# Projection, norm and router of layer one between the rounds of the second attention, a batch behind it

## The reference, cut to what matters

```python
scores = jnp.where(causal[None, None], scores, -jnp.inf)
...
attn = jax.nn.softmax(scores, axis=-1)
out = jnp.einsum('bhqk,bhkd->bqhd', attn, v).reshape(B, T, C)
return out @ w_out
...
x = _layernorm(x + _L1_attn_ref(x, ...), axis=-1)
...
xn = _rmsnorm(x_flat, norm_weight, EPS)
logits = xn @ router_weight.T + router_bias
probs = jax.nn.softmax(logits, axis=-1)
gate_vals, expert_idx = jax.lax.top_k(probs, TOP_K)
...
oh = jax.nn.one_hot(e_flat, E, dtype=jnp.int32)
pos = jnp.sum(jnp.cumsum(oh, axis=0) * oh, axis=-1) - 1
keep = pos < CAP
```

## Time and profile before

| | us |
|---|---|
| median of three runs | 2147.64 (2146.42 to 2150.34) |
| the profiled execution, its own time | 2137.1 |
| its span | 2135.4 |
| PE, DVE, ACT, POOL busy (share of the span) | 86%, 72%, 54%, 24% |
| mean granted clock of PE, share of full | 0.921 |

### The profile page before, as it was taken

How to read it: one execution, slowest core, us unless ns; L and a number is a source line. 1 busy time by engine, 2 the same in 40 slices (tenths; PEclk the granted TensorE clock), 3 DMA queues, 4 the chain that set the end, 5 groups by cost and what they waited for, 6 DMA issues and landing times. The chain is left out here.

```text
span 2135.4 us, 34245 instructions
## 1 busy us (share of the span) xinstructions
PE 1830.3 (86%) x12608; PEld 1134.4 (53%) x12608; DVE 1535.8 (72%) x2490; ACT 1149.6 (54%) x2279; POOL 511.6 (24%) x600
## 2 busy tenths in 40 slices
PE   5675899999999999699999879999987646999970
PEld 3342333333333333388888745555546535899860
DVE  7998999999999995366676455555526764666636
ACT  2330588888888889522322125555545543544526
POOL 3552152100000000132231112222211552333323
PEclk9995799999999999899999969999998757999985
DMA  3855437655334401123453374665624413443406
GB/s 120 240 204 131 110 55 186 189 140 85 66 52 81 71 13 39 59 71 99 148 149 109 138 183 109 140 150 140 174 86 150 146 65 120 141 140 126 153 28 232
DMA packets 165277, 258.19 MB, mean 121 GB/s; under 512 B 18398, under 2 KB 94083, under 8 KB 165136
## 3 DMA queue, kind: packets, MB, share of 16 engines
q1 hardware_dynamic: 137184, 191.11, 35.2%
q0 software_dynamic: 11696, 33.62, 4.3%
q10 hardware_dynamic: 16256, 31.59, 4.2%
HBM read 145.30 MB, written 108.92 MB: 119 GB/s over the span
## 5 line engine op out<-in xcount | busy, mean ns | idle before, releaser
L845 DVE TENSOR_REDUCE b_mx<-b_PM 128x2 f32<-128x1024 f32 x512 | 620.9, 1225 | 17.3 <-PE b_PM L701 13.5
L813 ACT ACTIVATE b_probs<-b_PS 128x512 f32<-128x512 f32 x1024 | 551.2, 598 | 79.3 <-PE b_PS L749 41.5
L1686 DVE TENSOR_REDUCE d_mx<-d_PM 128x2 f32<-128x1024 f32 (+1 forms) x192 | 178.1, 956 | 133.1 <-PE d_PM L1531 82.4
L1652 ACT ACTIVATE d_probs<-d_PS 128x512 f32<-128x512 f32 (+3 forms) x384 | 163.9, 498 | 150.9 <-PE d_PS L1579 150.5
L701 PE MATMUL b_PM<-b_kst,b_qst 48*128 48x512 f32 x512 | 185.0, 446 | 0.0
L749 PE MATMUL b_PS<-b_qst,b_kst 50*128 50x512 f32 x512 | 183.6, 454 | 0.7 <-ACT b_probs L813 0.7
L726 PE MATMUL b_PO<-b_probs,x_v 128*32 128x256 f32 x2048 | 164.9, 394 | 2.1 <-ACT b_outT L803 0.6
L726 PE MATMUL b_PO<-b_probs,b_vst 128*32 128x256 f32 x2048 | 163.2, 391 | 2.8 <-ACT b_outT L803 1.6
L2428 ACT ACTIVATE f_h<-f_PH,w_b 128x512 f32<-128x512 f32 x96 | 66.2, 689 | 139.5 <-PE f_PH L2387 129.2
L1626 POOL TENSOR_SCALAR_AFFINE_SELECT d_probs<-d_probs 128x128 f32<-128x128 f32 x256 | 71.8, 292 | 269.5 <-ACT d_probs L1652 262.8
L749 PEld LDWEIGHTS b_PS<-b_qst,b_kst 50*128 50x128 f32 x512 | 76.8, 184 | 108.4 <-ACT b_probs L813 92.3
(11 more groups left out here) (276 smaller groups left out, 3913.8 us busy)
## 6 DMA issues: line engine op xcount, KB each, us to landing
halves<-a_parts SPq DMA_DIRECT2D x7, 2048.0 KB, 8.5
qk<-c_halves ACTq DMA_DIRECT2D x7, 2048.0 KB
w_w<-L_ffn_fc1T SPq DMA_DIRECT2D x12, 1024.0 KB
w_w<-L_ffn_fc2T SPq DMA_DIRECT2D x12, 1024.0 KB, 5.5
d_qst<-qk SPq DMA_DIRECT2D x36, 256.0 KB, 5.1
d_kst<-qk SPq DMA_DIRECT2D x36, 256.0 KB, 7.2
slots<-b_zero POOLq DMA_DIRECT2D x16, 516.0 KB
v<-a_vaug ACTq DMA_DIRECT2D x32, 256.0 KB, 3.5
```

What stands on the lines that cost most here:

```text
L813: act.activation(probs[:, s % RING], PS[bank(s)][:], ACT.Exp).then_inc(exped, 1)
L845: dve.tensor_reduce(mx[:, :, p, qt, kh], PM[t % MTILES][:], AX.X, ALU.max)\
L1652: act.activation(probs[:, s % RING, 0:w], PS[bank(s)][:, 0:w], ACT.Exp).then_inc(exped, 1)
L1686: dve.tensor_reduce(mx[:, :, qt, kh], PM[t % MTILES][:, :, 0:keys(qt, kh)], AX.X, ALU.max)\
```

## The change

`phase_route` is gone. A new class `Routing` holds its work, cut into 66 ticks for each batch (`TICKS`), and `phase_attention1` runs one tick of it behind each round, on every engine. Batch b is routed from the first round of group 4(b+1) on, so one batch behind the attention; a tick k of batch b stands behind round k mod 12. Batch 3 has no rounds beside it: its 66 ticks run after the last round, with the last 18 ticks of batch 2. Three things change besides the place:

- The heads are divided by their sums channel-major, without turning them. SP sends row 32 of each head from `outT` to `totals` (`load_totals`), DVE takes the reciprocal (`invert_totals`), SP stores it to a new array `shares1` (`store_shares`) and loads it back, spread over the 32 channels, beside the sums (`load`); then one multiplication (`weigh`, POOL for batches 0 to 2, DVE for the last) and the projection. The 16 plus 8 transposes of a block before the projection are gone.
- A whole batch goes through each step of the chain, so there are half as many steps, on tiles twice as wide. The running count is a scan over tiles.
- The router's products and transposes go through `PM`, the two tiles of the maxima. And there are three stacks of queries and keys in place of four (`BUFS = 3`); the expert weights are loaded ahead in groups 5, 6, 9 and 10 in place of 6, 8, 12 and 14.

```diff
-    BUFS = HG1
+    BUFS = 3
...
+    LATE_TOTALS = (10, 6)
-    FIRST_WEIGHTS = {6: (0, True), 8: (0, False), 12: (1, True), 14: (1, False)}
+    FIRST_WEIGHTS = {5: (0, True), 6: (0, False), 9: (1, True), 10: (1, False)}
...
+class Routing:
+    STEPS = 24
+    TICKS = 66
+    WEIGH, WEIGH_LAST = (16, 18), (16, 20)
+    PROJECT = (18, 20)
+    STATS = (19, 20, 21, 22)
+    AGGR = (23, 24)
+    VARIANCE, ROOTS, DEVIATION = 25, 27, 28
+    NORM = 29
+    TURN = (31, 33)
+    SEND_COPY = 31
+    LOGITS, EXPS, RANKS = 34, 36, 46
+    SCATTER = 50
...
+    def load_totals(self, sp, outT, g, half):
+        if g > 0:
+            sp.wait_ge(self.shares_out[half], 16 * g)
+        for j in range(G1):
+            rows = slice(j * P // G1, (j + 1) * P // G1)
+            sp.dma_start(self.totals[rows, half], outT[j * VS1 + D1:j * VS1 + D1 + 1, half]).then_inc(self.totals_in[half], 16)
+
+    def store_shares(self, sp, d, g, half):
+        sp.wait_ge(self.totals_made[half], g + 1)
...
+        sp.dma_start(d["shares1"][heads, tok].rearrange("h (c n) -> h c n", n=self.CUTS), self.totals[:, half])\
+          .then_inc(self.shares_out[half], 16)
+
+    def load(self, sp, d, n, out_stored):
+        b, i, tok = n // HPS, n % HPS, slice(n * BLK, (n + 1) * BLK)
+        sp.wait_ge(out_stored[i], 16 * ((b + 1) * HG1 + 1))
+        sp.wait_ge(self.shares_out[i], 16 * (b + 1) * HG1)
...
+        for c in range(CD):
+            heads = slice(c * self.HEADS, (c + 1) * self.HEADS)
+            sp.dma_start(self.sums[:, i, c], sums[heads, 0:D1, tok]).then_inc(self.sums_in[i], 16)
+            share = d["shares1"][heads, tok].unsqueeze(1).to_broadcast([self.HEADS, D1, BLK])
+            sp.dma_start(self.shares[:, i, c], share).then_inc(self.sums_in[i], 16)
+        sp.dma_start(self.x2[:, i], d["x2"][tok, :].rearrange("(t p) c -> p t c", p=P)).then_inc(self.x2_in[i], 16)
...
+    def multiply(self, pe, ident, b, k):
+        if k in self.PROJECT:
+            n = b * HPS + self.PROJECT.index(k)
...
+            pe.wait_ge(self.weighed, n + 1)
+            self.free(pe, "project", n)
+            for t in range(TPK):
+                for c in range(CD):
+                    mm = pe.matmul(out[:, t // 2, t % 2 * DIM:(t % 2 + 1) * DIM], self.sums[:, n % HPS, c, t * P:(t + 1) * P],
+                                   self.wout[:, c, :], start=(c == 0), stop=(c == CD - 1))
+            mm.then_inc(self.projected, 1)
...
+    def invert_totals(self, dve, g, half):
+        dve.wait_ge(self.totals_in[half], self.TOTAL_DMAS * (g + 1))
+        dve.reciprocal(self.totals[:, half], self.totals[:, half]).then_inc(self.totals_made[half], 1)
+
+    def weigh(self, eng, n):
+        i = n % HPS
+        eng.wait_ge(self.sums_in[i], self.SUM_DMAS * (n // HPS + 1))
+        eng.tensor_tensor(self.sums[:, i], self.sums[:, i], self.shares[:, i], ALU.mult).then_inc(self.weighed, 1)
...
+    def send(self, pool, d, b, k):
+        if b < BATCH - 1 and k in self.WEIGH:
+            self.weigh(pool, b * HPS + self.WEIGH.index(k))
+        if self.SCATTER <= k < self.SCATTER + TPB * TOP_K:
...
+            pool.indirect_dma_start(out=d["slots"], out_offset=bass.IndirectOffsetOnAxis(
+                ap=self.to_slot[:, t, c:c + 1].bitcast(U32), axis=0), in_=self.xn[:, t], in_offset=None,
+                bounds_check=SLOTS - 1, oob_is_err=False).then_inc(self.scattered, 16)
...
             load(1)
             rows(0)
-            for g in range(2, BUFS):
-                load(g)
+            load(2)
+            route.load_weights(sp, d)
             for g in range(GROUPS):
...
                 store(g, 0)
+                if g > 0:
+                    route.store_shares(sp, d, g - 1, 1)
                 if g + 1 < GROUPS:
                     rows(g + 1)
+                if g > 0 and g % HG1 == 0:
+                    for i in range(HPS):
+                        route.load(sp, d, g // HG1 * HPS - HPS + i, out_stored)
+                route.store_shares(sp, d, g, 0)
+                if g == GROUPS - 1:
+                    route.load(sp, d, BLOCKS - HPS, out_stored)
                 store(g, 1)
                 if g + BUFS < GROUPS:
                     sp.wait_ge(pv_done, (g + 1) * ROUNDS + RING // G1)
                     load(g + BUFS)
...
-            for g in range(GROUPS):
-                for i in range(ROUNDS):
-                    slot(g, i)
-            for r in range(ROUNDS - PAIRED, ROUNDS):
-                values(GROUPS - 1, r)
+            for T in range(TICKS):
+                if T < GROUPS * ROUNDS:
+                    slot(T // ROUNDS, T % ROUNDS)
+                if T == GROUPS * ROUNDS:
+                    for r in range(ROUNDS - PAIRED, ROUNDS):
+                        values(GROUPS - 1, r)
+                for b, k in Routing.at(T, PER_BATCH):
+                    route.multiply(pe, ident, b, k)
```

More of the change, by code:

```diff
@@ L1386, in phase_attention1 @@
+def phase_attention1(nc, d, keep, weights, tokens, shared):
     K = len(PAIRS1) * D1
     KM = K + HALVES1
-    BUFS = HG1
+    BUFS = 3
     GROUPS = BATCH * HG1
@@ L1425, in phase_attention1, with groups_left, maximum_at @@
     MASKS = masks_through(ROUNDS - 1)
+    def groups_left(g):
+        return min(2, GROUPS - 1 - g)
+    PER_BATCH = HG1 * ROUNDS
+    TICKS = GROUPS * ROUNDS + Routing.TICKS
+    def maximum_at(T):
+        if T < GROUPS * ROUNDS:
+            g, ahead, t = T // ROUNDS, 1 + (AHEAD + T % ROUNDS) // STEPS, (AHEAD + T % ROUNDS) % STEPS
+            if ahead <= groups_left(g):
+                return g + ahead, t
+    ring = [("max", 0, t) for t in range(STEPS)] + [("max", 1, t) for t in range(AHEAD)]
+    for T in range(TICKS):
+        if now := maximum_at(T):
+            ring.append(("max", *now))
+        for b, k in Routing.at(T, PER_BATCH):
+            ring.extend(Routing.entries(b, k))
+    entry = {name: n for n, name in enumerate(ring)}
     with ExitStack() as ctx:
@@ L2261 @@
-ROUTE_STEPS = 24
+            for T in range(TICKS):
+                if now := maximum_at(T):
+                    take(*now)
+                    if now[1] == STEPS - 1:
+                        minus_max(now[0])
+                g, i = T // ROUNDS, T % ROUNDS
+                if g < GROUPS and i == LATE_TOTALS[0]:
+                    route.invert_totals(dve, g, 0)
+                if 0 < g <= GROUPS and i == LATE_TOTALS[1]:
+                    route.invert_totals(dve, g - 1, 1)
+                for b, k in Routing.at(T, PER_BATCH):
+                    route.choose(dve, b, k)
@@ L2656, in program @@
             tokens = Routed(nc, layer1)
-            with ExitStack() as routing:
-                incoming = Unrouted(nc, routing)
-                phase_attention1(nc, d, keep, weights, incoming, shared)
-                phase_route(nc, d, keep, weights, incoming, tokens)
+            phase_attention1(nc, d, keep, weights, tokens, shared)
             phase_experts(nc, d, keep, weights)
```

852 lines of the change are left out of this document (368 added, 484 removed).

## The result

The changed kernel takes 2277.2 us (median of four, 2269.7 to 2279.9) against 2147.0 for the kernel before on the same chip. The ratio, its time over that of the kernel before, is 1.060, with a 95% interval of 1.057 to 1.063. It is slower by 130 us, where the forecast was 78 and the range ended at 2275. Its profiled execution took 2276.8 us, 139.7 more than that of before.

What follows compares the result with a forecast made beforehand. PE, busy 39.54 of 40 us in the attention rounds, was taken as the bound. Terms -187 + 82 + 41 + 82 + 43 + 17 = +78 took the profiled 2137.1 to 2215, so 2225 us was expected; range 2155 to 2275.

Steps and rivals of the forecast that it cites:

- The sign and its mechanism: Whole kernel: slower, chance 0.87, with PE waiting 13 times in round 6 for queries or keys and its clock falling.
- The rival in which the change is faster: Round 6 waits only 3.5 us each, 45 in all, too short to move the clock: -9, 2138 us; chance 0.12.
- the one in which the clock stays up: PE's clock does not fall after the round 6 waits: +35, 2182 us, still slower; chance 0.20.
- The rival in which the clock stays down: PE at half clock through most of each of 13 groups, losing 7.5 us instead of 3.3: 2280 us; chance 0.09.
- The removed stage, 187: phase_route, from PE's last value product to the experts' first load, disappears: -186.9 us.
- The tail, 82: Behind the last round, batch 3 is routed with nothing beside it: +82 us, bounds 72 to 92.
- Four loads issued at 0.6 and about 4 until 1 MB has landed: 6.4: Step of the tail: batch 3's loads ahead of the multiplication, 6.4 us.
- PE work, 41: Between the rounds, router projections, turns, logits and rank products take PE 13.8 us per batch, three batches: +41 us.
- Waits, 82: Round 6 of groups 3 to 15: PE waits 6.3 us for late queries and keys, 13 times: +82 us.
- Crowding, 17: Batch loads delaying keys (8), plus scatters and chain steps PE waits on in order (9): +17 us, bounds 0 to 30.
- 2 to 3 us late, three times: Step of crowding: keys delayed behind a batch's 3 MB, 13 us at 225 GB/s, in groups 4, 8 and 12: 8 us.
- The clock, 43: PE's clock falls after each of 13 round 6 waits, costing 3.3 us each: +43 us; bounds 0 to 4 each.

Runs made afterwards that it cites:

- spread loads alone: The changed kernel with a block's sums and shares loaded by head in eight DMAs of 32 x 2 x 512 instead of four: 2222.6 us, ratio 1.046.
- the run with early keys: The changed kernel with queries and keys of group g+3 requested at group g's last score, ahead of its second stored half: 2203.5 us, ratio 1.036.
- three stacks alone: The kernel before with three stacks of queries and keys in place of four, nothing else changed: 2227.1 us, ratio 1.048.
- work in the waits: The kernel before with three stacks and 24 useless PE products ahead of each wait for queries and keys: 2208.5 us, ratio 1.041.
- the two runs that moved it: Changed kernel, spread loads, early keys in halves, batch loads behind group g+3's values; ticks from multiplication four or eight rounds later: ratios 0.994 and 0.999.
- the first run with the loads behind the keys: Changed kernel, spread loads, early keys in halves, batch loads behind group g+3's values, ticks from multiplication four rounds later: 2132.0 us, ratio 0.994.

## Why the prediction was right and wrong

The sign and its mechanism were right: 13 waits at round 6, of 6.4 us in ordinary groups where 6.3 was taken, a clock at 0.50 behind every one, and groups of 27 to 30 us where no batch is routed (29 to 31 was forecast). The rival in which the change is faster falls with them, and so does the one in which the clock stays up. The rival in which the clock stays down has 2280, next to the 2277 measured, but by luck: the clock was back 3.5 to 7.1 us after each wait, and the missing time lay elsewhere.

Term by term, against the profiled difference of 139.7:

- The removed stage, 187: so in the traces compared, but 164 on other chips.
- The tail, 82: measured 101.0, outside the bounds of 72 to 92. The failed step is "Four loads issued at 0.6 and about 4 until 1 MB has landed: 6.4", and the store ahead of it, which was put at 1.5 with two DMAs of sums. The loads took 14.8 us to the multiplication, and the last stored half, behind the previous block's loads, took 5.65 to issue by itself. Spread, the tail was 85.5, inside the bounds.
- PE work, 41: the products have the durations of the earlier trace rows. Projection 3.67, turn 1.09, logits 3.72 for a batch at full clock, in the run with early keys.
- Waits, 82: ten of 6.4, and the three behind a batch at 6.4 would be 83. Right.
- Crowding, 17, of which 8 for "2 to 3 us late, three times": this is the step that failed. The three waits are 67.8 in place of 19.2, 48.6 more, beyond the bound of 30. The step took the rate of the earlier trace rows, 225 GB/s, for DMAs of another shape, and 0.6 us for each issue. They moved at about 100 GB/s with the DMA engines 26% busy, and their issues grew to 1 to 4 us, in one place to 7.5. With the loads spread, the three waits exceed 6.4 by 7.8 in all, where the step had 8: its account of the bytes was right, for DMAs of the other shape.
- The clock, 43: at most 29.6 with three stacks alone, 2.3 per wait in place of 3.3, of which work in the waits gave 20.9 back. In the changed kernel 217.2 - 131.9 - 41 = 44 is left of the rounds for the clock and the chain steps, where 43 + 9 was forecast. The Trainium skill, TensorE: Matmul & The Clock Gate, section "HAM oscillation — how this bites in real kernels", has the cost of the fall paid at every burst, and the trace agrees: 13 of 13.

Of the 62 us missing (139.7 less 78), 40 are the three waits (48.6 less 8) and 19 the tail. Both have one cause: spread loads alone took 41 off the three waits and 15.5 off the tail. The 8.4 outside the two stretches and the 8 less for the clock and the chain cancel by chance.

## What to carry to other kernels

When a buffer is dropped, ask in which round its next load can be issued and in which it is needed; with three stacks the rounds were 101 us longer or 3 by that alone. A transfer has a rate by its shape, not by its bytes: price one of a new shape from a row of that shape, and where a DMA's outer dimension is 4, look at the engines' busy share while it runs. A big load delays whatever stands behind it in the queue, and in the two runs that moved it another wait came for each that went.

## What the runs showed of the hardware

An issue on SP's queue, mostly 0.4 to 0.6 us, took up to 7.5 us (a load of shares at 1556 in the changed kernel). The shape is not all of it: behind eighteen spread loads an issue of the maxima's rows still took 4.0 to 5.3 us in the first run with the loads behind the keys. Four small facts beside it: useless products of 5.7 us in a wait made the kernel 19 us faster, by the clock; the clock fell to 0.50 at the 32 products of 128x16 of the logits, three times in each of nine traces, with PE busy; the same kernel's router stage takes 164 or 187 us by chip; and the loads of keys, with all engines busy, move 209 to 250 GB/s, where 373 were reached in another stage.
